# Expert layer: gate and up products issued alternately, with the transposes of the former unit's activations ahead of both

## The reference

```
x = layernorm(x)
probs = softmax(x @ w_gate.T);  top 4 of 16 -> routing_weight
g = x @ wg[e];  u = x @ wu[e];  act = silu(g) * u
routed = sum over e of routing_weight * (act @ wd[e])
shared = silu(x @ sg) * (x @ su) @ sd
out = routed + shared
```

## Time and profile before

| | |
|---|---|
| median of three runs | 2082.15 us (2081.03 to 2084.95) |
| profiled execution, first to last instruction (span) | 2116.1 us, the only time that the profile gives for it |
| mean granted TensorE clock | 0.948 |
| TensorE matmul busy | 1856.6 us, 88% |
| TensorE weight load busy | 1416.6 us, 67% |
| VectorE, ScalarE, GpSimd busy | 1179.0, 928.3, 963.2 us |
| DMA | 412.51 MB, mean 195 GB/s |

### The profile page before, as it was taken

How to read it: one execution, slowest core, us unless ns; L and a number is a source line. 1 busy time by engine, 2 the same in 40 slices (tenths; PEclk the granted TensorE clock), 3 DMA queues, 4 the chain that set the end, 5 groups by cost and what they waited for, 6 DMA issues and landing times. The chain is left out here.

```text
span 2116.1 us, 38662 instructions
## 1 busy us (share of the span) xinstructions
PE 1856.6 (88%) x11487; PEld 1416.6 (67%) x11487; DVE 1179.0 (56%) x2617; ACT 928.3 (44%) x2627; POOL 963.2 (46%) x1011
## 2 busy tenths in 40 slices
PE   4588999999986988999999999995789999886992
PEld 1355665665555877899999999994356656545882
DVE  5566776776653755333333344333777877764445
ACT  3367676776651322223333333331266666641110
POOL 1477777787631235213333333432365454311561
PEclk9999999999988989999999999997899999996996
DMA  8578877788725325569999988644344444529657
GB/s 323 183 228 280 259 234 228 238 274 242 225 93 195 100 46 146 164 178 269 295 304 295 287 249 241 171 86 103 83 93 110 114 104 113 121 68 389 230 164 273
DMA packets 231727, 412.51 MB, mean 195 GB/s; under 512 B 45083, under 2 KB 119196, under 8 KB 226213
## 3 DMA queue, kind: packets, MB, share of 16 engines
q1 hardware_dynamic: 165164, 322.28, 48.2%
q0 software_dynamic: 30592, 62.08, 12.8%
q10 hardware_dynamic: 35776, 25.69, 4.3%
HBM read 211.97 MB, written 155.52 MB: 174 GB/s over the span
## 5 line engine op out<-in xcount | busy, mean ns | idle before, releaser
L705 ACT ACTIVATE a_P<-a_SC,a_nm 128x256 f32<-128x256 f32 x512 | 235.9, 473 | 131.1 <-DVE a_nm L607 129.8
L1223 POOL DMA_INDIRECT b_y_rows<-b_ysb,b_entry x79 | 124.5, 1576 | 334.3 <-ACT b_ysb L1371 186.6
L607 DVE TENSOR_REDUCE a_nm<-a_SC 128x2 f32<-128x512 f32 x256 | 164.8, 685 | 139.1 <-PE a_SC L838 139.1
L570 POOL TENSOR_TENSOR a_praw<-a_praw,a_phigh 128x704 f32<-128x704 f32 (+2 forms) x126 | 192.6, 1528 | 10.3
L1475 DVE TENSOR_TENSOR b_xl<-b_XT,b_xh 128x512 fp32r<-128x512 f32 x97 | 67.1, 691 | 210.3 <-ACT b_xh L1377 205.8
L849 PEld LDWEIGHTS a_T<-ident,a_P 128*128 128x128 f32 x1024 | 119.1, 144 | 80.2 <-issue 51.6
L849 PE MATMUL a_T<-ident,a_P 128*128 128x128 f32 x1024 | 145.6, 281 | 21.8 <-DVE a_PT L619 16.2
L1382 ACT ACTIVATE b_ah<-b_AT 128x384 fp32r<-128x384 f32 x111 | 54.6, 492 | 230.9 <-PE b_AT L1307 174.9
L1481 DVE TENSOR_TENSOR b_al<-b_AT,b_ah 128x384 fp32r<-128x384 f32 x111 | 61.9, 558 | 168.1 <-ACT b_ah L1382 145.3
L568 POOL CAST a_phigh<-a_praw 128x704 fp32r<-128x704 f32 (+2 forms) x126 | 111.1, 882 | 96.7 <-DMA a_praw<-in_L_ffn_wd 34.1
L2202 ACT ACTIVATE c_P<-c_SC,c_nm 128x240 f32<-128x240 f32 x256 | 115.7, 457 | 76.6 <-DVE c_P L2074 76.6
(11 more groups left out here) (492 smaller groups left out, 4936.6 us busy)
## 6 DMA issues: line engine op xcount, KB each, us to landing
w_parts<-a_phigh SPq DMA_DIRECT2D x72, 352.0 KB
w_parts<-a_praw SPq DMA_DIRECT2D x72, 352.0 KB, 3.8
b_wh<-w_parts SPq DMA_DIRECT2D x18, 1216.0 KB
b_wl<-w_parts SPq DMA_DIRECT2D x18, 1216.0 KB
c_q<-c_qT SPq DMA_DIRECT2D x64, 256.0 KB
c_k<-c_kT SPq DMA_DIRECT2D x124, 128.0 KB
b_wh<-w_parts SPq DMA_DIRECT2D x18, 704.0 KB
b_wl<-w_parts SPq DMA_DIRECT2D x18, 704.0 KB
```

The costliest lines, as they stand in the source:

```text
L570: eng.tensor_tensor(raw[:, 0:k * m], raw[:, 0:k * m], r32(high[:, 0:k * m]), ALU.subtract).then_inc(plow_done, 1)
L607: eng.tensor_reduce(nm[:, g % 4, j, :], SC[j][:, :].rearrange("p (t k) -> p t k", t=BT), AX.X, ALU.max, negate=True).then_inc(topped, 1)
L705: e = eng.activation(Pr[:, i, t, :], SC[j][:, t * S:(t + 1) * S], ACT.Exp, bias=nm[:, g % 4, j, t:t + 1], accum_out=den[:, h, t:t + 1])
L1223: eng.indirect_dma_start(out=y_rows, out_offset=bass.IndirectOffsetOnAxis(ap=entry[:, r, 1:2].bitcast(U32), axis=0), in_=ysb[:, v % RING, ...
```

## The change

The two functions for gate and up products become one, which waits for everything that both waited for and then issues, for each of the twelve pairs of token block and weight block, the gate matmul and right behind it the up matmul with the same token block. The counter of the gate products is raised by the last gate matmul, the next to last matmul of the unit. The transposes of the former unit's activations are issued ahead of this pair of products, where they used to stand between gate and up. Nothing changes on the other engines.

```
             def gate_and_up_products(v):
                 weights_at(v)
                 if v == 0:
                     eng.wait_ge(gw_ready, 2)
                 eng.wait_ge(x_lo, turns(v))
                 ge(eng, silu_done, v - 1)
+                if v < DENSE:
+                    eng.wait_ge(rest_in[v // NT], 64)
+                ge(eng, act_done, v)
                 n = GE if v < NT else I
                 i = 0
                 high, low = token_parts(v)
                 for x_, w_ in ((high, wh), (high, wl), (low, wh)):
                     for k in range(KD):
-                        m = eng.matmul(G[v % 2][:, 0:n], x_[:, k, :], gate_cols(w_, at_unit[v], k, n),
-                                       start=(i == 0), stop=(i == 3 * KD - 1))
-                        i += 1
-                m.then_inc(g_done, 1)
-
-            def up_products(v):
-                if v < DENSE:
-                    eng.wait_ge(rest_in[v // NT], 64)
-                ge(eng, act_done, v)
-                ...
-                        m = eng.matmul(U[:, 0:I], x_[:, k, :], up_cols(w_, at_unit[v], k),
-                                       start=(i == 0), stop=(i == 3 * KD - 1))
+                        first, last = i == 0, i == 3 * KD - 1
+                        g = eng.matmul(G[v % 2][:, 0:n], x_[:, k, :], gate_cols(w_, at_unit[v], k, n), start=first, stop=last)
+                        if last:
+                            g.then_inc(g_done, 1)
+                        m = eng.matmul(U[:, 0:I], x_[:, k, :], up_cols(w_, at_unit[v], k), start=first, stop=last)
                         i += 1
                 m.then_inc(up_done, 1)
...
                     turn_tokens(u + 2)
-                if 0 <= u + 1 < NU:
-                    gate_products(u + 1)
                 if u >= 0:
                     turn_acts(u)
                 if 0 <= u + 1 < NU:
-                    up_products(u + 1)
+                    gate_and_up_products(u + 1)
                 if u >= 0:
                     down_products(u)
```

More of the change, by code:

```diff
@@ L1272, in weights_at, with gate_and_up_products @@
                 eng.wait_ge(routed_in, needed)
-            def gate_products(v):
+            def gate_and_up_products(v):
                 weights_at(v)
```

## The result

The changed kernel takes 2116.85 us (median of four runs, 2113.43 to 2120.42), the kernel before 2083.55 us on the same chip (four runs, 2081.03 to 2085.04). The ratio is 1.0167, 95% interval 1.0143 to 1.0192: 33 us slower, where 5 us had been forecast and 2093 us was the upper end of the range. The sign was right, the size was not.

What follows compares the result with a forecast made beforehand. The prediction took TensorE's order of work and waits in the expert layer as the bound. Start +3.65 and table loads +1.4 gave +5.05 us, all else zero: 2087.2 us from 2082.15, range 2077 to 2093.

Steps and rivals of the forecast that it cites:

- What bounds the kernel: Expert layer: TensorE busy 766.8 of 810 us, so only its order of work and its waits can move the end.
- Alternation taken as zero: Gate and up matmuls in turn: no change in cost; bounds 50 us gained to 5.3 us lost.
- The silu's lost cover: Gate's reading no longer beside up products; by the skill's strict rule silu's 0.46 us stands open in each unit.
- The seven transposes in one group: Token and activation transposes now together still cost 0.44 and 0.32 us, so a unit stays 6.7 us.
- The activation chain: Activation transposes may start 1.19 us after S, the down products' start; TensorE arrives at S + 2.49, slack 1.3 us.
- The new wait for the activations ahead of the gate products: Met by the transposes' wait just before, so the 79 routed units of 111 lose nothing.
- Where the slack is gone: Silu table reloads make the chain 2.61 us: units 6 and 10 late 0.12, 14 and 18 late 0.56; +1.4 us.
- The start: Stage start: one wait for both weight halves delays gate 0, down products later by 3.65 us, bounds +2.4 to +7.
- Rival 1: Stops ahead of down products, mostly near GpSimd's scatters, shrink with earlier activations: 10 us less, 2077 us; chance 0.14.
- Rival 2: Slower by operand order, 2 ns a matmul, or by a chain passing 2.49 us in routed units: 2092 us; chance 0.14.
- Rival 3: Start costs nothing lasting, the stage's first units catch up at a later stop: +1 us, 2083 us; chance 0.06.
- Rival 4: Alternation removes the fixed part of each gate and up matmul: 40 us less, 2047 us; chance 0.04.

Runs made afterwards that it cites:

- e3: Changed kernel with next unit's register loads ahead of the activation transposes and all gate products before all up products; 0.9997 of the kernel before.
- e10: Changed kernel with next unit's register loads ahead of the activation transposes and gate and up alternating by four; 1.0005 of the kernel before.
- e1: Changed kernel with only the next unit's register loads moved ahead of the activation transposes; 2087.27 us, 1.0032 of the kernel before.
- e2: Changed kernel with twelve gate products, then twelve up products, register loads still behind the activation transposes; 2084.24 us, 1.0030 of the kernel before.
- e8: Kernel before with only the activation transposes moved ahead of the gate products, up alone waiting for the second weight half; 0.9980 of the kernel before.
- e6: Changed kernel with register loads ahead of the activation transposes, plus one unused register load there per routed unit; 1.0027 of the kernel before.
- e5: Changed kernel plus one unused register load per routed unit, behind the waiting activation transposes; 2171.34 us, 1.0442 of the kernel before.
- e9: Changed kernel with four gate, eight alternating gate-up pairs, four up, and register loads ahead of the activation transposes; 0.9996 of the kernel before.

## Why the prediction was wrong

*What bounds the kernel: TensorE's order and waits.* Right, but read too narrowly. I took TensorE to be its array. Its instruction stream is a second resource with a length of its own, and no busy time of the page shows it.

*Alternation taken as zero, bounds of -50 and +5.3 us.* Against kernels that have everything but the alternation one by one (e3, e10) it was at the upper bound: 2 ns a matmul, 0.05 us a unit, 5 us over 111 units by the traces; e1 against e3 gives 7 us. So zero was 5 us short. Against the kernel before, whose gate and up products both start 161 ns apart, the ordinary unit didn't get longer (6.71 us in e1, 6.72 before), only because the next item gives back as much. The silu's lost cover, which the prediction put at up to 0.46 us a unit, cost the array nothing directly, since the transposes waited in no routed unit. But the later end of gate moved the activations by 0.4 us, and by e2 that is what made the loads late.

*The seven transposes in one group cost the same.* Nearly right: e3's ordinary unit is 6.66 us against 6.72 of the kernel before, 0.055 x 111 = 6 us less, and e8 has the 4 us in its times. By the medians over 75 routed units, half of the 0.055 is in the up products, 159 ns apart instead of 161, and half in the down products (2.06 us instead of 2.09). Why they are closer there is open.

*The activation chain: may start at S + 1.19, slack 1.3 us.* The chain was right to 0.04 us (the loads start at S + 1.23) and the array's slack was right too: the transposes never waited in a routed unit. This is why the error isn't in the arithmetic.

*"The new wait for the activations ahead of the gate products is met by the wait of the transposes just before. Routed units, 79 of 111: nothing."* This is the step that failed. The sentence is true of the array. What I didn't ask is which instructions of TensorE itself stand between the two waits. The diff moves `gate_products`, whose first statement is `weights_at`: two register loads with a check each, 1.7 us of stream up to the first weight load. They used to be ahead of the transposes' wait and now stand behind it. The correct sum is S + 1.2 for the wait plus 1.7 for the stream = S + 2.9 at the first gate product, against S + 2.05 + 0.44 + 0.25 = S + 2.74 for the array: 0.16 us an ordinary unit, 12 to 13 us over 79, and the slow loads on top, the rest of the 27. The loads of lines 1270 and 1271 should have had a term in the sum; the prediction doesn't mention them.

*Where the slack is gone: +1.4 us.* Units 6 and 10 were forecast late by 0.12 us and their transposes came 0.15 us later than in their neighbours (S + 2.66 against 2.51). Units 14 and 18, without token transposes ahead, were forecast at 0.56 each. Unit 14's transposes come at S + 2.79, where 2.07 is usual without token transposes, so 0.72; 18 shows none. Sum 1.0 us, a little under the forecast. Unit 12 loses another 0.57 (S + 3.08 against 2.51) for a reason that had no term: ScalarE took up its gate products 1.87 us after their end.

*The start: +3.65 us.* The changed kernel, all engines:

```profile
658.07 0.64 PE L1289 MATMUL b_G<-b_wh 128*128 128x368 f32 x1 [9.38 <-DMA b_wl<-w_parts]
...
663.40 0.18 ACT L1379 ACTIVATE b_lg<-b_G 128x16 f32<-128x16 f32 x1 [14.07 <-PE b_G L1289]
663.59 1.28 ACT L1380 ACT_TABLE_LOAD   x1
664.88 0.46 ACT L1380 ACTIVATE b_silu<-b_G 128x352 f32<-128x352 f32 x1
...
665.45 0.53 DVE L1495 TENSOR_TENSOR b_act<-b_U,b_silu 128x352 f32<-128x352 f32 x1 [15.11 <-ACT b_silu L1380]
...
666.03 0.55 PE L1300 MATMUL b_AT<-ident,b_act 128*128 128x128 f32 x3 [2.07 <-DVE b_act L1495]
```

One wait for both halves, then 2.67 us from the end of the products (663.36) to the transposes, forecast 2.61, and the down products at 670.36, forecast 4.32 us later and found at 4.33. From the first transposes of the stage (641.89) to there it is 28.5 us, against 25.4 before: +3.1. Right for this trace; in the other kernels with one wait and alternation this stretch is 28.8 to 32.1 us. That it goes through to the end is only partly borne out (e8 against e3).

*The rivals.* Rival 1 (the down products' stops shrink) rests on stops that the trace of before had and its runs had not; in the eleven later traces the dense units take 6.7 to 6.9 us in the mean, in the one of before 8.0. So there was nothing to win. I had set that against it, rightly. Rival 2 had the right sign and named both the 2 ns and a chain that passes its slack, but it put the late chain down to ScalarE at a map conversion, and in the routed units ScalarE and VectorE were on time (S + 1.17). Rival 3 isn't decided: what of the start lasts to the end was told apart by e3 and e8 alone, 1.0 us in the traces and 3.5 in the ratios. Rival 4 is refuted by the spacing of 161 to 163 ns.

*The whole.* Late gate products 27, alternation 5, start 3, table loads 1, up and down products -6: 30 us of 33. The other 3 are within the spread of the runs. Without the late gate products it would have been some +3 us, near the forecast of 5, with luck in it, since the alternation and the -6 nearly cancel.

## What to carry to other kernels

When a block is moved behind a wait, list all that the engine itself executes for it, register loads and address arithmetic too: an engine has a stream and a datapath, and a wait that costs the datapath nothing can cost the stream all its lead. Put loads that give addresses ahead of the first wait on recent work; it cost nothing here (e6), and moving one call gave back 28 us (e1). The sign of such a case in a profile is a datapath wait with no releaser ("issue") ahead of the same instruction each time, with an engine that counts as busy as before.

## What the runs showed of the hardware

- A register load on TensorE took 0.296 us at least and 0.307 in the middle (line 1270 of the changed kernel), up to 1.28 in the slowest there and 1.59 on line 1271 of e5, and the whole step with its check 0.64 us. Of the 158 loads of lines 1270 and 1271, 21 to 24 took over 0.6 us in the kernel before and where they stand behind the waiting transpose, 33 to 49 in e1, e3, e6, e8, e9 and e10, where they stand ahead of it and cost nothing. Why they are slow is open. The Trainium skill ("DMA: Bandwidth & Descriptors", section Latency and other measured facts) gives about 0.6 us as the least for a `tensor_load`. By the traces the load is half of that, and the step of load and check is what comes to 0.6.
- The loads started 0.06 us after the activations that a transpose ahead of them waited for, in all 79 routed units of the changed kernel, and in the unit shown 1.3 us before that transpose ran. So what stands behind a waiting transpose is held by its semaphore, and not by its turn on the array. The Trainium skill ("TensorE: Matmul & The Clock Gate", section Architectural detail) says that TensorE's queue can pull weight loads ahead of matmuls in flight. The trace fits it: in the changed kernel the first weight load of a down product and the up matmul ahead of it both start at 745.63. No run here shows that a register load passes a waiting instruction.
- Matmuls of 352 columns start 161 and 163 ns apart when they alternate between two banks one by one (changed kernel, e1), 161 (gate) and 159 (up) in e3 and e10, and 161 and 161 in the kernel before. What makes the 2 ns is open.
- What held the loads at S - 0.27 us in the kernel before and S - 0.8 in e1, rather than earlier, wasn't tried.
